# Left-over rows of the second feed-forward product: two tiles multiplied side by side in 64-row halves of TensorE

## What is computed

```
h = layernorm(x) * (1 + ca) + sa
x = x + ga * linear_attention(h)                 # first phase, "A"
h = layernorm(x) * (1 + cb) + sb
for l in 0, 1:                                   # second phase, "L": DEPTH = 2 layers
    q, k, v = split(shift_token(h) @ wqkv[l])    # 8 heads of 64
    q, k = rotary(l2norm(q) * qs), rotary(l2norm(k) * ks)
    h = h + local_attention(q, k, v) @ wo[l]     # each block of 128 rows sees itself and the one before
    y = layernorm(shift_token(h)) * lg + lb
    a, g = split(y @ w1[l] + b1[l])              # 682 columns each
    h = h + (a * gelu(g)) @ w2[l] + b2[l]        # the product that the change touches
x = x + gb * h
```

## Time and profile before

| | |
|---|---|
| median of 3 runs | 3249.38 us (3248.24 to 3250.14) |
| the profiled execution | 3245.92 us, its span 3244.1 us |
| mean granted TensorE clock | 0.991 of full speed |
| busy: PE, DVE, POOL, ACT | 97%, 82%, 79%, 66% of the span |
| chain that ended last | PE 91%, POOL 3%, issue 2%, DVE 2% |
| phase A, then phase L on PE | to about 595 us, then from 603 us |

### The profile page before, as it was taken

One profiled execution on the slowest core, in us unless ns is written; L12 is line 12 of the kernel. 1 busy time (PEld: TensorE's weight loads), 2 busy tenths in 40 slices (PEclk: granted clock), 3 DMA queues, 4 the chain that ended last, 5 costly groups with the idle time before them and its releaser, 6 DMA issues.

```text
span 3244.1 us, 85014 instructions
## 1 busy us (share of the span) xinstructions
PE 3139.3 (97%) x25436; PEld 2434.1 (75%) x25436; DVE 2654.7 (82%) x8312; ACT 2146.4 (66%) x5372; POOL 2575.4 (79%) x2892
## 2 busy tenths in 40 slices
PE   5999999699999999999999999999999999999998
PEld 3677677467777777777777777777777777777777
DVE  5899999578777777777777788888888888888885
ACT  3656666367767676767676777776767676767674
POOL 3999999687777777777777778888888888888885
PEclk8999999899999999999999999999999999999999
DMA  6211111000000000000000001111111111111111
GB/s 217 80 46 48 49 46 47 29 21 24 24 25 24 25 24 25 24 25 24 25 24 25 24 25 37 37 37 38 37 38 37 38 37 38 37 38 37 38 37 30
DMA packets 153077, 125.03 MB, mean 39 GB/s; under 512 B 22580, under 2 KB 149032, under 8 KB 152368
## 3 DMA queue, kind: packets, MB, share of 16 engines
q1 hardware_dynamic: 146352, 110.67, 11.2%
q10 hardware_dynamic: 6272, 8.93, 0.9%
HBM read 77.51 MB, written 42.02 MB: 37 GB/s over the span
## 4 chain that ended last, share of the span: by engine, by line
PE 91%; POOL 3%; issue 2%; DVE 2%; ACT 1%; DMA 1%; ACTq 0%; SPq 0%; DVEq 0%; POOLq 0%
PE bank L541 33%; PE bank L737 19%; PE bank L745 10%; PE bank L548 9%; PE bank L710 7%; PE bank L689 6%; PE bank L604 2%; PE bank L622 2%; POOL shared L1269 1%; PE bank L584 1%; PE bank L587 1%; PE bank L633 1%; PE bank L615 1%; DMA X<-in_x 0%; PE bank L723 0%
## 5 line engine op out<-in xcount | busy, mean ns | idle before, releaser
L737 PEld LDWEIGHTS bank<-zT,W 128*128 128x128 f32 x5632 | 667.1, 192 | 137.2 <-issue 134.8
L1305 POOL TENSOR_TENSOR rnorm<-clamped,HALF 128x8 f32<-128x8 f32 x256 | 420.5, 1643 | 413.7 <-DVE clamped L1135 407.2
L541 PE MATMUL bank<-WQKV,xT 128*128 128x512 f32 x1536 | 743.5, 607 | 5.3 <-DVE rotary_work L1118 4.4
L737 PE MATMUL bank<-zT,W 128*128 128x128 f32 x5632 | 671.0, 275 | 13.7 <-issue 11.7
L1318 POOL TENSOR_TENSOR shared<-shared,share_of 128x512 f32<-128x512 f32 x512 | 585.3, 1171 | 59.3 <-DVE shared L1170 59.3
L906 ACT ACTIVATE shared<-shared,negmax 128x256 f32<-128x256 f32 x1024 | 505.6, 495 | 27.2 <-DVE negmax L1154 25.7
L541 PEld LDWEIGHTS bank<-WQKV,xT 128*128 128x128 f32 x1536 | 263.8, 192 | 216.1 <-issue 214.0
L1132 DVE TENSOR_REDUCE sums<-rotary_work 128x8 f32<-128x512 f32 x256 | 175.5, 685 | 287.5 <-ACT rotary_work L876 283.7
L1170 DVE COPY_PREDICATED shared<-BEYOND,shared 128x256 f32<-128x256 int32 x512 | 400.0, 793 | 0.0
L1154 DVE CUSTOM_DVE_ANT_0 shared<-bank,MASK 128x256 f32<-128x256 f32 x1024 | 365.8, 420 | 0.1
L1328 POOL TENSOR_TENSOR shared<-shared,IDENT 128x256 f32<-128x256 f32 x512 | 362.4, 729 | 0.0
(11 more groups left out here) (153 smaller groups left out, 6638.3 us busy)
## 6 DMA issues: line engine op xcount, KB each, us to landing
X<-xl_rows SPq DMA_DIRECT2D x128, 128.0 KB, 2.2
X<-in_x SPq DMA_DIRECT2D x64, 128.0 KB, 2.1
x_tiles<-ax SPq DMA_DIRECT2D x64, 128.0 KB, 1.7
xl_rows<-axl SPq DMA_DIRECT2D x64, 128.0 KB, 1.7
XS<-xl_rows SPq DMA_DIRECT2D x128, 64.0 KB, 2.1
xm_rows<-X SPq DMA_DIRECT2D x128, 64.0 KB, 1.6
xs<-xm_rows SPq DMA_DIRECT2D x128, 64.0 KB, 1.8
xl_rows<-X SPq DMA_DIRECT2D x64, 128.0 KB, 1.7
```

Of the source, the lines that this page charges most:

```text
L541: mm = nc.tensor.matmul(held(tile, key)[:, 0:cols], lhsT[c], rhs[c], start=(c == 0), stop=(c == len(lhsT) - 1))
L737: mm = nc.tensor.matmul(held(tile, key)[:, k * P:(k + 1) * P], W1[:, tile.l, c, at:at + P], zT[:, c], start=(c == 0), stop=(c == KC - 1))
L1305: G.tensor_tensor(rnorm[q][:], clamped[q][:], HALF[:].to_broadcast((P, LH)), ALU.pow).then_inc(done[f"root_{key}"], 1)
```

## The change

- `narrow` multiplies only the five full chunks for each tile and then counts up `narrowed`. In an odd slot it also multiplies the left-over rows of the even tile before and of its own: two products of 64 rows, one in rows 0 to 63 of the array and one in rows 64 to 127, each into the bank of its tile. Then `nw_filled` goes up by 2.
- `gate` writes the left-over rows of an even tile to rows 0 to 41 of `hid_tail` and those of an odd tile to rows 64 to 105. The 42 rows of `W2` are loaded twice, at rows 0 and 64.
- `gate` waits for `narrowed` of the tile before, and gate2 also for `nw_filled` of two tiles before.
- `add_f` does nothing for an even tile and both tiles for an odd one.
- `ORDER_L` is another table, `BANK_A` and `BANK_L` are others too; `ORDER_A` is the same. `narrow` is at depth 4 on PE, `finish` and `store` at 6, `project_v` at 1, `project_o` at 2, `weigh1` apart from the other three.

```
-                for m in range(HC):
-                    mm = nc.tensor.matmul(held(tile, "nw")[:, 0:D], hid[:, m] if m < HC - 1 else hid_tail[:], W2[:, tile.l, m],
-                                          start=(m == 0), stop=(m == HC - 1))
-                mm.then_inc(filled["nw"], 1)
+                for m in range(HC - 1):
+                    mm = nc.tensor.matmul(held(tile, "nw")[:, 0:D], hid[:, m], W2[:, tile.l, m], start=(m == 0), stop=False,
+                                          skip_group_check=True)
+                mm.then_inc(done["narrowed"], 1)
+                if tile.s % 2 == 1:
+                    for s in (tile.s - 1, tile.s):
+                        rows = slice(s % 2 * LD, s % 2 * LD + LD)
+                        mm = nc.tensor.matmul(bank[int(BANK_L["nw"][s])][:, 0:D], hid_tail[rows], W2[rows, tile.l, HC - 1],
+                                              start=False, stop=True, skip_group_check=True)
+                    mm.then_inc(filled["nw"], 2)
...
-                load(W2[0:LAST, l, HC - 1], w2[l, FULL:HID])
+                for e in range(2):
+                    load(W2[e * LD:e * LD + LAST, l, HC - 1], w2[l, FULL:HID])
...
-                after(dve, filled["nw"], tile, back=1)
+                after(dve, done["narrowed"], tile, back=1)
+                if m == HC // 2 - 1:
+                    after(dve, filled["nw"], tile, back=2)
...
+                tail = tile.s % 2 * LD
...
-                    to = hid[:, k] if k < HC - 1 else hid_tail[0:LAST]
+                    to = hid[:, k] if k < HC - 1 else hid_tail[tail:tail + LAST]
...
             def add_f(tile):
+                if tile.s % 2 == 0:
+                    return
                 after(dve, filled["nw"], tile)
                 after(dve, done["add_b2"], tile)
-                V.tensor_tensor(X[tile.s][:], X[tile.s][:], held(tile, "nw")[:, 0:D], ALU.add).then_inc(done["add_f"], 1)
+                for s in (tile.s - 1, tile.s):
+                    V.tensor_tensor(X[s][:], X[s][:], bank[int(BANK_L["nw"][s])][:, 0:D], ALU.add).then_inc(done["add_f"], 1)
```

One pair of rows of the order table, the rest being of the same kind:

```
-    "SP": [(0, "load"), (3, "shift"), (3, "late"), (5, "store")],
+    "SP": [(0, "load"), (5, "late"), (6, "store"), (2, "shift")],
```

More of the change, by code:

```diff
@@ L63 @@
 ORDER_L = {
-    "SP": [(0, "load"), (3, "shift"), (3, "late"), (5, "store")],
[L65 to L69, removed]
[5 rows of a table removed]
-           (2, "diagonal3"), (4, "add_b2"), (0, "root_k"), (0, "add_k"), (0, "scale_k"), (3, "root_x"), (5, "finish"),
-           (1, "share0"), (1, "share1"), (1, "share2")],
+    "SP": [(0, "load"), (5, "late"), (6, "store"), (2, "shift")],
+    "PE": [(4, "widen1"), (4, "widen2"), (2, "turn_p0"), (1, "project_v"), (1, "turn_q"), (0, "turn_x"), (2, "weigh1"),
+           (2, "turn_p1"), (0, "project_k"), (3, "turn_z_first"), (1, "ready_score"), (3, "turn_z_last"), (1, "score"),
+           (2, "weigh2"), (2, "weigh3"), (2, "weigh0"), (3, "widen0"), (2, "project_o"), (0, "turn_k"), (0, "project_q"),
+           (4, "narrow")],
+    "ACT": [(0, "age_k"), (4, "gelu"), (1, "keep_v"), (0, "keep_x"), (1, "keep_q"), (3, "norm"), (0, "square_k"),
[3 rows of a table added]
+           (1, "invert1"), (2, "add_o"), (1, "invert2"), (0, "sum_q"), (0, "rotate_q")],
+    "POOL": [(1, "root_q"), (1, "scale_q"), (2, "share2"), (2, "share3"), (2, "diagonal2"), (2, "diagonal3"), (3, "root_x"),
+           (3, "add_b2"), (6, "finish"), (0, "root_k"), (0, "add_k"), (0, "scale_k"), (1, "share0"), (1, "share1"),
+           (1, "diagonal0"), (1, "diagonal1")],
 }
 BANK_A = {
-    "av": "27475705", "kv": "01010161", "num": "52642746", "az": "33333333", "kphi": "52642540", "cum": "74757652",
-    "sc0": "10101616", "sc1": "52642740", "sc2": "74757052", "sc3": "65264274", "aqk": "33333333", "awo": "10151610",
-    "aq": "52642640",
+    "av": "61024104", "kv": "41024102", "num": "66662246", "az": "33333333", "cum": "10241746", "kphi": "57575057",
+    "sc2": "24105610", "sc3": "57572757", "sc0": "10241046", "sc1": "66666224", "aqk": "33333333", "awo": "10241024",
+    "aq": "57575757",
 }
 BANK_L = {
[4 rows of a table removed]
[3 rows of a table added]
 }
@@ L111 @@
              "add_q", "summed_q", "sum_q", "max0", "max1", "max2", "max3", "invert0", "invert1", "invert2", "invert3", "add_o",
-             "stats", "norm", "gate", "add_f", "add_k", "root_k", "scale_k", "root_q", "scale_q", "share0",
+             "stats", "norm", "gate", "narrowed", "add_f", "add_k", "root_k", "scale_k", "root_q", "scale_q", "share0",
              "share1", "share2", "share3", "root_x", "add_b2", "gated", "finish", "weigh0", "weigh1", "weigh2", "weigh3", "other_mask",
@@ L318, in adaln_block @@
         consts_ready, factors_ready, rows_moved = sem("consts_ready"), sem("factors_ready"), sem("rows_moved")
-        WEIGHT_LOADS, LAYER_LOADS = 7, 12 * DEPTH + 6
+        WEIGHT_LOADS, LAYER_LOADS = 7, 13 * DEPTH + 6
         ROWS_STORED = 2 * DEPTH + 1
```

## The result

| | before | changed kernel |
|---|---|---|
| median | 3248.81 us (4 runs, 3245.75 to 3250.14) | 3367.64 us (4 runs, 3366.20 to 3369.41) |
| ratio | | 1.037, 95% interval 1.0356 to 1.0383 |
| profiled execution, span | 3245.92, 3244.1 | 3366.20, 3364.3 |
| mean granted TensorE clock | 0.991 | 0.981 |

The change makes the kernel 3.7% slower.

A forecast was written before the change was run, and what follows sets the result against it. Inside the layers PE's queue was taken as the bound, at their ends the latency of chains through other engines. Steady slots +22.0, fill +2.3 and drain -10.7 gave +13.6 on 3249.4: 3263.0 us, range 3245 to 3292.

The forecast's parts named there:

- the loop: PE, once in eight slots where the loop branches: some 1.2 us idle, expected unchanged.
- What is late next: Even slots: ready_score, claiming p1's bank, waits for keep_p1; the tightest wait, fitting by 0.3 us if DVE is free.
- Rival C: Steady even slots: two add_f delay keep_p1 on DVE, 0.54 us in 64 slots, +35 us, 3298; chance 0.17.
- Steps 1 to 3: PE's steady slots: pair gains 0.06 a slot, weigh1 apart costs 0.24, together +0.18 over 122 slots, +22.0 us.
- D: Left-over pair: its halves do not run side by side, +26.2 us, 3289; chance 0.05.
- excursion: weigh1 alone on PE: entering and leaving the narrow shape once more costs 0.09 and 0.15, +0.24 us a slot.
- Rival A: PE's array: changing shape costs nothing, so slots shrink by 0.216 us, 3214.6 us; chance 0.10.
- Step 4: Pipeline's ends, a slot shorter on PE: fill 93 us, +2.3; drain 67.5 us, -10.7.
- Rival B: Pipeline's ends and first phase: fill slots of 15 us and a smoother first phase, 13 us more gain, 3250; chance 0.13.
- Step 5: Other edits, such as W2's second load and the first phase's bank table: 0, with 5 us either way.

The follow-up runs named there:

- experiment 10: Changed kernel with the loops of VectorE, TensorE, ScalarE and GpSimd written out and gate0 and gate1 ahead of keep_p0: 3269.63 us, 1.0077 of the kernel before.
- experiment 9: Kernel before with the layer-phase loops of VectorE, TensorE, ScalarE and GpSimd written out: 3230.36 us, 0.9956 of the kernel before.
- experiment 1: Changed kernel with VectorE's layer-phase loop written out, same work in the same order: 3297.95 us.
- experiment 2: Changed kernel with gate0 and gate1 ahead of keep_p0 in VectorE's order, gate2 behind it: 3346.71 us.
- experiment 7: Kernel before with project_v put between weigh0 and weigh1, one more change of the array's shape in each slot: 3289.22 us.

## Why the prediction was wrong

The difference in the 122 slots, closed by the runs:

| part | from | us |
|---|---|---|
| PE's work | experiment 10 minus 9 | +34.7 |
| wait of the odd slots | experiment 1 minus 10, 61 odd slots | +13.6 |
| first slot of each block | experiment 1 minus 10, 61 even slots | +9.7 |
| ends of the block, after | changed kernel minus experiment 1 | +73.0 |
| ends of the block, before | experiment 9 minus before | -16.3 |
| sum | measured 114.7 | +114.7 |

The first row is a comparison of two kernels. The third is most likely what the branches of the other three engines leave; experiment 10 takes away these and puts the gates first, so the two are not separated.

**The step that failed: the loop.** "Once in eight slots, where the loop branches, PE idles some 1.2 us for nothing that the profile shows", and: "I expect that unchanged." I took a gap that I saw on PE for a property of PE. Each engine has its own branch, and the change moved DVE's from ahead of a step with 2 to 4 us of slack (sum_q; the sums wait 78 us for ACT in the earlier trace rows) to ahead of invert3, with stats and add_f behind it and none. The new table said so in its first and last entries. No rival had this mechanism. It cost 73.0 - 16.3 = 56.7 us, or 66.4 with the first slots of the blocks. The sum fell 106.6 short on the span: 56.7 here, 9.7 in those first slots, 13.6 in the odd ones, 12.7 of work (34.7 for 22.0), 5.4 in the fill, 10.2 in the drain, less 1.7 ahead of phase L.

**What is late next.** "The tightest wait is ready_score, which in even slots claims the bank of p1." It was turn_p1 in odd slots, on the bank of `ag0`, for the gates of the same slot: 0.30 us in 61 slots, 18.5 us by experiment 2 (13.6 once VectorE's loop is written out). I had taken this bank for one drained long ago, though widen0 is at depth 3 and gate at depth 4, and gate stands behind keep_p0. Rival C had the engine right (DVE) and the place and the size (some 35 us) wrong: no wait for keep_p1 shows in the long stretch.

**Steps 1 to 3, PE's work: right in kind, a term too small.** The halves run side by side (D is out), and entering and leaving cost what I read for the groups themselves: the pair 0.64 and 0.09, and the excursion's first 0.24. What I left out is the 0.10 on the first full-array instruction behind a narrow group (0.06 where that is a transpose). So the pair saves 0.03 rather than 0.12, weigh1 costs 0.30 rather than 0.24, and a slot +0.29 rather than +0.18: 34.7 us and not 22.0. Rival A, the shape for nothing, is out. The rule of the Trainium skill, "TensorE: Matmul & The Clock Gate", section "Measured speedup vs the span model", would make the pair 0.43; the rows of experiment 10 have 0.83, with the price of the shape on both sides.

**Step 4, the ends: wrong.** Its sums are slightly off as well: 93 in place of 90.9 is +2.1 and not +2.3, and 57.4, 4 and 5.9 are 67.3 and not 67.5. The fill came to 98.6 in place of 93: 20.4, 17.9, 19.5, 19.2 and 21.6, so the slots that I put at 17 to 18.4 were 1.3 longer on average, and the last had the odd slot's work and wait. The drain gave 0.5 and not 10.7. PE's work there was about as counted, 57.9 for 57.4, but PE waited 10.5 us in place of 4 (in the kernel before it had waited 7.8 there), ran some 2.7 us longer (the granted clock was 0.85 from 3330 to 3345 us), and 6.4 lay behind the start of the last pair. Three of those waits:

```profile
3325.64 0.66 PE L709 MATMUL bank<-shared,vring 128*64 128x128 f32 x8 [1.47 <-DVE shared L1187]
...
3345.26 0.33 PE L547 MATMUL bank<-IDENT,z 128*128 128x128 f32 x1 [2.05 <-ACT z L925]
...
3355.51 2.43 PE L744 MATMUL bank<-W,shared 128*128 128x256 f32 x10 [1.58 <-DVE hid_tail L1220]
```

My reading, which no run tests: a shorter pipeline has fewer tiles in flight at its end to cover each other's chains, and I had priced the missing work and not the missing cover. Rival B is out.

**Step 5, the first phase.** I had 0 with 5 either way; it was 1.7 shorter.

What stays open: whether the pair could pay in the order of before. Between two full-array steps it saves 0.03 us a pair, so little hangs on that; beside a step that is narrow already (score, weigh) the change of shape might cost less, which no run tries. The pair wasn't tried alone: in the bank table of before the left-over bank of an even tile would be claimed again before the odd tile's slot has filled it. Why a branch shows as 2.4 us in one place and 5 in another isn't settled either.

## What to carry to other kernels

Before you price a new order for several engines, write down for each engine which step comes first behind its loop's branch and how long that step used to wait: here a branch cost nothing where that wait was longer, and some 6 us of the kernel's time where there was none. Take every claim of a buffer to the step that counts it free, with slot and place in that engine's queue, and not only the one that looks tightest. When narrow pieces of the array are laid side by side, add the change of shape on both sides: for 0.43 us of work it took back all but 0.03 of what it saved.

## What was not expected of the hardware

- In the twelve ends of a block, over all these runs, a loop's branch shows on VectorE as 2.3 to 5.8 us without an instruction, on TensorE as 0.6 to 1.5, on ScalarE as 1.2 to 2.2. Written out, all of them are gone, and the kernel before gains 0.44%.
- A group that uses 64 columns or 64 rows of the array has a price outside itself: 0.09 us on the instruction ahead and 0.10 on the one behind (1.91 for 1.72 in experiment 7).
- After the waits at a block's end the granted clock was 0.50 for some 3 us, and PE's next groups took up to twice their time: behind two waits of 4.9 us together came 1.6 us more of work. In layer 1 it was the same behind waits of 0.5 and 2.3 us (granted 0.50 from 2294 to 2296 us).
